# Shares of layer-2 tiles per chunk, and which tiles of the last stretch are split, in a two-layer graph kernel

## The chip, the cores and the metric

The kernel runs on one core of one Trainium2 chip. The metric is the device time of one execution in microseconds (us); the median of three runs is given. Changes of about 0.2% of it (some 3.7 us) can be told from none.

## What is computed

`x` is 8192 x 128, `adj` 8192 x 8192, all f32. The reference, cut to what matters:

```
h = relu(layernorm(x))
h1 = h @ W + B
mask = (adj < 0.5) & ~eye
S = where(mask, exp(-(1/adj - 1/mu)**2 / (2*sigma**2)), 0)
x = x + S @ h1                                   # layer 1
h2 = relu(layernorm(x)) @ W1.T
x = x + (adj*adj + eye) @ h2                     # layer 2
```

## The kernel before

**Tiles.** The 8192 rows are 16 chunks of 512. `adj` is read as 16 x 16 tiles (row chunk, source chunk), each 128 partitions x 2048 f32, 1 MB. A tile is used in layer 1 and in layer 2. Layer 2 of a tile (row, source) needs `h2` of its source chunk, and that is known only when layer 1 of that chunk is done, so most tiles are loaded twice. A tile is four steps of 128 rows on TensorE (PE); a plain f32 matmul stands in the trace as two records, so a plain tile is eight.

**Steps and chunks.** Step s = 16 c + i is the i-th layer-1 tile of chunk c; there are 256 such steps (LAST = 240 is the first of the last chunk), and then 34 more with layer-2 tiles alone. The 256 layer-2 tiles ("items", numbered m = 0 to 255 in the order in which every engine does them) are put beside the steps. `QUOTA[c]` (L31) says how many items go beside chunk c; the last chunk takes what is left. `make_plan` (L86) spreads them over the 16 steps of the chunk and collects them in chains: tiles of one row that add up in one PSUM bank, which VectorE (DVE) then copies out (`add_chain`, L722) and GpSimd (POOL) adds to the output by DMA. In the last chunk three items stand beside most steps, in some steps two.

**A layer-1 tile.** DVE masks it (`premask`, L607, the instruction at L619), ScalarE (ACT) takes log (L801) and reciprocal (L806), DVE squares (L626), ACT takes the exponential (L811), and PE multiplies three steps later (`l1`, L440, L449). In the last chunk `premask(t)` waits until PE has done `l1(t-3)`, because the ring of results has three places there.

**A layer-2 tile.** Its entries are squared in place, by DVE (L637) or ACT (L819; in the last chunk always ACT), and PE multiplies by `h2` (L483). A diagonal tile also gets the unit matrix added by DVE (L604).

**Split tiles.** In the last stretch some items are split by DVE into a high part (L658) and a low part (L660, both in `halves`, L648); PE then does three fast matmuls for each step of 128 rows (L461 to L463, twelve records for a tile) in place of the plain ones. `SPLITS` (L172) chooses them by a rule of the index:

```
SPLITS = [it for it in ITEMS if it.step >= LAST + SPLIT_STEP.get(it.source, STEPS) and it.row != it.source
          and it.m % 7 not in (1, 4)]
```

DVE splits item m when it comes to item m+1. So the last item of a step is split in the next step, behind that step's `premask`:

```
for it in AT_STEP[s]:
    if dense and it is AT_STEP[s][0]:
        premask(s)
    ...
    if it.m and ITEMS[it.m - 1].split is not None:
        halves(ITEMS[it.m - 1])
```

PE goes through step s as `l1(s-3)`, then the items of step s-1. At the start of a chunk `centre_row(c-1)` (L518) stands behind the chunk's first `l1`; it waits for `add_x1(c-1)` on DVE (L696), which is queued behind a square and a `premask` of that step.

**Loads.** SP loads tiles in the order of use into a ring of eight places; a place is free when PE is done with the item that was in it.

Of the kernel before, what the change touches and what calls it, by code (L numbers as in the profile page):

```python
# [27 lines left out]

QUOTA = [0, 11, 13] + [12] * 3 + [13] * 9  # L31
S_STEPS = NC * NC
H2_STEP = 6

# [3 lines left out]
LAST = S_STEPS - NC  # L38
# [6 lines left out]
SPLIT_STEP = {10: 3, 11: 3, 13: 5, 12: 7, 14: 12, 15: 16}  # L45
# [22 lines left out]
def slots_of(c):  # L68

    if c == 1:  # L70
        n = QUOTA[1]
        first = H2_STEP - 1
        return [first + k * (NC - first) // n for k in range(n)]
    if c < NC - 1:
        n = QUOTA[c]
        return [(2 * k + 1) * NC // (2 * n) for k in range(n)]
    n = NC * NC - 2 * NC + 1 - sum(QUOTA) - len(KEPT)
    return [(2 * k + 1) * NC // (2 * n) for k in range(n)]
# [70 lines left out]
CHAINS, ITEMS, ORDER = make_plan()  # L149
STEPS = ITEMS[-1].step + 1  # L150
# [8 lines left out]
for s in range(STEPS):  # L159
# [3 lines left out]
    for it in AT_STEP[s]:  # L163
# [3 lines left out]
        else:  # L167
# [1 line left out]
            LOADS.append((None, it))  # L169


SPLITS = [it for it in ITEMS if it.step >= LAST + SPLIT_STEP.get(it.source, STEPS) and it.row != it.source  # L172
          and it.m % 7 not in (1, 4)]
for it in ITEMS:
    it.split = None
for r, it in enumerate(SPLITS):
    it.split = r
# [62 lines left out]
def gnn_program(nc, xT, adjT, W0, B0, mu, sigma, W1T, outT):  # L240
    with ExitStack() as ctx:
# [332 lines left out]
        def _(dve):  # L574
# [74 lines left out]
            def halves(it):  # L649
# [6 lines left out]
                else:  # L656
                    dve.wait_ge(q_used, SPLITS[it.split - 3].m + 1)
                dve.tensor_copy(high[:, :], squares).then_inc(high_ready, 1)  # L658
# [295 lines left out]
```

## Time and profile before

| | us |
| --- | --- |
| median of 3 runs (1869.32 to 1871.13) | 1870.15 |
| the profiled execution | 1871.51 |
| its span, first to last instruction | 1869.6 |
| PE busy | 1835.1 (98%) |
| DVE busy | 1743.2 (93%) |
| ACT busy | 1731.2 (93%) |
| DMA, mean over the span | 271 GB/s |

All times of the rows below are from the start of the span. "Busy" of PE is taken with matmuls that overlap and with modelled ends; the distance from start to start of two records is the surer measure of what one costs.

### The profile page before, as it was taken

Reading aid. Unit: us, or ns where it says so; the run is one execution under the profiler, and the core shown is the slowest. Engines: PE = TensorE matmul, PEld = TensorE weight load, DVE = VectorE, ACT = ScalarE, POOL = GpSimd, SP = SyncE. Lnnn points to the kernel's source line nnn. Section 1 sums busy time; section 2 is a strip of 40 time slices with the busy share of each in tenths; the row PEclk is TensorE's granted clock in tenths of the full one; section 3 lists DMA queues with packets and bytes.
Section 4 is the critical chain, followed back from the end, with each engine's and each line's share of the span. In section 5 each row is a group of like instructions: output and inputs, shape, how many; then the busy total and the mean of one; then the engine's idle time right before and its main releaser. Section 6 shows DMA issues by size and latency. Waiting matters only on the chain.

```text
span 1869.6 us, 13360 instructions
## 1 busy us (share of the span) xinstructions
PE 1835.1 (98%) x4836; PEld 884.6 (47%) x4836; DVE 1743.2 (93%) x1029; ACT 1731.2 (93%) x985; POOL 96.1 (5%) x118
## 2 busy tenths in 40 slices
PE   7989999999999999999999999999999999999998
PEld 4544444444444444444444444444444444555665
DVE  7999999999999999999999998999999994778796
ACT  8999899999999999999999999999999998888664
POOL 0000000000000000000000000000000000000111
PEclk9999999999999999999999999999999999999999
DMA  8476889897978787777878776676756678866998
GB/s 315 162 288 257 319 305 308 288 324 246 330 267 316 261 298 278 276 279 275 284 263 304 237 247 241 249 255 228 255 200 232 232 265 297 291 253 229 311 339 250
DMA packets 85297, 507.29 MB, mean 271 GB/s; under 512 B 9840, under 2 KB 10480, under 8 KB 28144
## 3 DMA queue, kind: packets, MB, share of 16 engines
q1 hardware_dynamic: 69840, 476.68, 67.0%
q0 software_dynamic: 15248, 29.63, 9.2%
q8 instruction: 39, 0.64, 0.1%
q14 instruction: 26, 0.21, 0.0%
q10 hardware_dynamic: 144, 0.13, 0.0%
HBM read 476.51 MB, written 29.88 MB: 271 GB/s over the span
## 4 chain that ended last, share of the span: by engine, by line
PE 76%; DVE 11%; ACT 8%; issue 3%; DMA 1%; SPq 0%; DVEq 0%
PE p_x L483 21%; PE p_l1b L449 20%; PE p_l1a L449 15%; PE p_own L483 11%; DVE rings L626 4%; DVE rings L619 3%; ACT rings L801 3%; DVE rings L637 2%; ACT rings L811 2%; ACT rings L806 2%; PE p_l1a L483 1%; PE p_x L461 1%; PE p_x L462 1%; PE p_x L463 1%; PE p_own L461 1%
## 5 line engine op out<-in xcount | busy, mean ns | idle before, releaser
L619 DVE SCALAR_TENSOR_TENSOR rings<-rings 128x2048 f32<-128x2048 f32 x256 | 584.6, 2284 | 35.9 <-PE p_l1b L449 31.0
L626 DVE SCALAR_TENSOR_TENSOR rings<-rings,small 128x2048 f32<-128x2048 f32 x256 | 599.9, 2344 | 14.4 <-ACT rings L806 14.2
L811 ACT ACTIVATE rings<-rings,small 128x2048 f32<-128x2048 f32 x256 | 533.1, 2082 | 47.0 <-DVE rings L626 46.5
L801 ACT ACTIVATE rings<-rings,small 128x2048 f32<-128x2048 f32 x256 | 509.6, 1991 | 15.3 <-DVE rings L619 11.6
L483 PE MATMUL p_x<-rings,h 128*128 128x512 f32 x1144 | 513.3, 592 | 0.0
L806 ACT ACTIVATE rings<-rings 128x2048 f32<-128x2048 f32 x256 | 488.0, 1906 | 5.6
L449 PE MATMUL p_l1b<-rings,h 128*128 128x512 f32 x1024 | 461.2, 596 | 0.0
L449 PE MATMUL p_l1a<-rings,h 128*128 128x512 f32 x1024 | 458.4, 593 | 0.7 <-DVE h L687 0.7
L483 PEld LDWEIGHTS p_x<-rings,h 128*128 128x128 f32 x1144 | 216.8, 190 | 266.3 <-issue 264.8
L637 DVE TENSOR_TENSOR rings<-rings 128x2048 f32<-128x2048 f32 x136 | 310.4, 2282 | 1.6
L449 PEld LDWEIGHTS p_l1b<-rings,h 128*128 128x128 f32 x1024 | 195.2, 191 | 240.7 <-issue 237.6
L449 PEld LDWEIGHTS p_l1a<-rings,h 128*128 128x128 f32 x1024 | 193.1, 190 | 235.7 <-issue 233.4
L819 ACT ACTIVATE rings<-rings 128x2048 f32<-128x2048 f32 x120 | 224.8, 1900 | 38.3 <-DMA rings<-adjT 28.1
L483 PE MATMUL p_own<-rings,h 128*128 128x512 f32 x520 | 233.6, 592 | 0.0
L920 POOL DMA_DIRECT2D outT<-xa_buf x97 | 82.5, 853 | 1422.0 <-DVE xa_buf L737 1409.4
L483 PEld LDWEIGHTS p_own<-rings,h 128*128 128x128 f32 x520 | 98.6, 190 | 120.0 <-issue 119.5
L660 DVE TENSOR_TENSOR low<-rings,high 128x2048 fp32r<-128x2048 f32 x41 | 94.0, 2292 | 1.4
L737 DVE COPY xa_buf<-p_x 128x512 f32<-128x512 f32 x86 | 58.6, 682 | 17.2 <-PE p_x L483 17.2
L658 DVE CAST high<-rings 128x2048 fp32r<-128x2048 f32 x41 | 50.0, 1221 | 12.4 <-ACT rings L819 12.4
L461 PE MATMUL p_x<-high,h_high 128*128 128x512 f32 x92 | 41.4, 450 | 0.5 <-DVE low L660 0.5
L463 PE MATMUL p_x<-high,h_low 128*128 128x512 f32 x92 | 35.9, 390 | 0.0
L462 PE MATMUL p_x<-low,h_high 128*128 128x512 f32 x92 | 35.9, 390 | 0.0
(92 smaller groups left out, 571.0 us busy)
## 6 DMA issues: line engine op xcount, KB each, us to landing
rings<-adjT SPq DMA_DIRECT2D x446, 1024.0 KB, 6.9
outT<-xa_buf POOLq DMA_DIRECT2D x97, 256.0 KB, 7.3
x_buf<-xT SPq DMA_DIRECT2D x24, 256.0 KB, 6.4
outT<-y_buf POOLq DMA_DIRECT2D x15, 256.0 KB, 7.5
xa_buf<-xT SPq DMA_DIRECT2D x8, 256.0 KB, 5.6
outT<-x_buf POOLq DMA_DIRECT2D x1, 256.0 KB, 5.0
y_buf<-outT SPq DMA_DIRECT2D x1, 256.0 KB, 12.6
outT<-y_buf SPq DMA_DIRECT2D x1, 128.0 KB, 1.8
```

The source lines that it names most:

```text
L449: last = pe.matmul(p_l1[c % 2][:, :], h1[:, J * G + g, :], block_of(s_ring, slot_of(t), g), start=(i == 0 and g == 0), stop=(i == NC - 1 a ...
L461: pe.matmul(out[:, :], h_high, high, start=(it.first and g == 0), stop=False)
L483: last = pe.matmul(out[:, :], h2[:, it.source * G + g, :], block_of(a_ring, it.load % A_RING, g), start=(it.first and g == 0), stop=(it.la ...
L619: dve.scalar_tensor_tensor(out=tile(s_ring, slot_of(t)), in0=tile(a_ring, slot), scalar=CUTOFF, in1=tile(a_ring, slot), op0=ALU.is_lt, op1 ...
L626: dve.scalar_tensor_tensor(out=v, in0=v, scalar=neg_2c, in1=v, op0=ALU.add, op1=ALU.mult).then_inc(squared, 1)
L637: squares = dve.tensor_tensor(a, a, a, ALU.mult)
L660: dve.tensor_tensor(low_ring[it.load % A_RING][:, :], squares, high[:, :].bitcast(F32), ALU.subtract).then_inc(low_ready, 1)
L801: act.activation(v, v, ACT.Ln, bias=tiny_c).then_inc(ln_done, 1)
L806: act.activation(v, v, ACT.Exp, scale=-1.0).then_inc(recip_done, 1)
L811: act.activation(v, v, ACT.Exp, bias=exp_bias, scale=neg_k).then_inc(sens_done, 1)
L819: squares = act.activation(a, a, ACT.Square)
L920: pool.dma_start(columns(outT, ch.row), xa_buf[ch.index % XA_RING][:, :], accum_op=how).then_inc(xa_stored[ch.index % XA_RING], 16)
```

## The change

```
-QUOTA = [0, 11, 13] + [12] * 3 + [13] * 9
+QUOTA = [0, 11, 13, 11, 14, 12, 14, 12, 13, 13, 12, 14, 12, 12, 12]
...
-SPLITS = [it for it in ITEMS if it.step >= LAST + SPLIT_STEP.get(it.source, STEPS) and it.row != it.source
-          and it.m % 7 not in (1, 4)]
+MAY_SPLIT = [it for it in ITEMS if it.step >= LAST + SPLIT_STEP.get(it.source, STEPS) and it.row != it.source]
+WHICH = "SSSSSSSSSSS.SSS..SSSS.SS.S.SSSSSS.S.SS.S.SS.SSSS.SS.SSSSSS"
+SPLITS = [it for it, w in zip(MAY_SPLIT, WHICH) if w != "."]
```

Chunk 3 gets 11 items for 12, chunk 4 14 for 12, chunk 6 14 for 13, chunk 7 12 for 13, chunk 10 12 for 13, chunk 11 14 for 13, chunks 12, 13 and 14 each 12 for 13, and the last chunk 47 for 45. 45 tiles are split in place of 41: 22 for 18 beside the last chunk's steps (seven for four in steps 243 to 247, fifteen for fourteen in steps 248 to 255), and 23 in both kernels in the 34 steps behind it, at other places. There are 97 chains for 98. Lines behind L172 stand one further down.

The first place is DVE in steps 253 and 254. L619 (now L620) is `premask`, L626 (L627) the square of a layer-1 tile, L658 and L660 (L659, L661) the high and the low part of a split tile, L604 (L605) a unit matrix, L737 (L738) a copy of a chain. Before, from the `premask` of step 253:

```order
L619 SCALAR_TENSOR_TENSOR rings<-rings 128x2048
L658 CAST high_57<-rings 128x2048
L660 TENSOR_TENSOR low_51<-rings,high_57 128x2048
L626 SCALAR_TENSOR_TENSOR rings<-rings,small 128x2048
L619 SCALAR_TENSOR_TENSOR rings<-rings 128x2048
L658 CAST high_58<-rings 128x2048
L660 TENSOR_TENSOR low_52<-rings,high_58 128x2048
L658 CAST high_59<-rings 128x2048
L660 TENSOR_TENSOR low_55<-rings,high_59 128x2048
L737 COPY xa_buf<-p_l1a 128x512
L658 CAST high_57<-rings 128x2048
L660 TENSOR_TENSOR low_54<-rings,high_57 128x2048
```

The changed kernel, from the `premask` of step 253:

```order
L620 SCALAR_TENSOR_TENSOR rings<-rings 128x2048
L605 TENSOR_TENSOR rings<-rings,eye 128x4x128
L659 CAST high_58<-rings 128x2048
L661 TENSOR_TENSOR low_52<-rings,high_58 128x2048
L659 CAST high_59<-rings 128x2048
L661 TENSOR_TENSOR low_51<-rings,high_59 128x2048
L627 SCALAR_TENSOR_TENSOR rings<-rings,small 128x2048
L620 SCALAR_TENSOR_TENSOR rings<-rings 128x2048
L738 COPY xa_buf<-p_l1a 128x512
L659 CAST high_57<-rings 128x2048
L661 TENSOR_TENSOR low_55<-rings,high_57 128x2048
L659 CAST high_58<-rings 128x2048
```

Before, step 253 has two items, the last of them split: its parts are the first pair behind the `premask` of step 254, followed by the pairs of that step's own two split items. Now step 253 has three items, the last of them plain, and behind the `premask` of step 254 come a copy and the pairs of that step's own items.

The second place is DVE at steps 262 to 266, in the part without layer 1. L703 (L704), L710 (L711), L668 and L670 (L669, L671) belong to the layer norm and `h2` of the last chunk. Before, from that layer norm's first row:

```order
L703 TENSOR_SCALAR normed_buf<-p_stat 128x512
L658 CAST high_57<-rings 128x2048
L660 TENSOR_TENSOR low_50<-rings,high_57 128x2048
L710 TENSOR_TENSOR h<-p_proj,rstd_columns 128x512
L668 CAST h_high_70<-h 128x512
L670 TENSOR_TENSOR h_low_71<-h,h_high_70 128x512
L658 CAST high_58<-rings 128x2048
L660 TENSOR_TENSOR low_52<-rings,high_58 128x2048
L658 CAST high_59<-rings 128x2048
L660 TENSOR_TENSOR low_53<-rings,high_59 128x2048
L737 COPY xa_buf<-p_x 128x512
L658 CAST high_57<-rings 128x2048
```

The changed kernel, from the same row:

```order
L704 TENSOR_SCALAR normed_buf<-p_stat 128x512
L659 CAST high_58<-rings 128x2048
L661 TENSOR_TENSOR low_50<-rings,high_58 128x2048
L659 CAST high_59<-rings 128x2048
L661 TENSOR_TENSOR low_51<-rings,high_59 128x2048
L711 TENSOR_TENSOR h<-p_proj,rstd_columns 128x512
L669 CAST h_high_70<-h 128x512
L671 TENSOR_TENSOR h_low_71<-h,h_high_70 128x512
L659 CAST high_57<-rings 128x2048
L661 TENSOR_TENSOR low_53<-rings,high_57 128x2048
L738 COPY xa_buf<-p_x 128x512
L659 CAST high_58<-rings 128x2048
```

Before, the pairs behind the layer norm are those of items 227, 229, 230 and 231 (steps 261, 263, 264, 265). Now they are those of items 227, 228, 230 and 232 (steps 261, 262, 264, 266): two pairs stand ahead of `h2` for one, and items 229 and 231 are plain.

## Rows read from the trace of the kernel before

**Rows 1.** Page: busy time and share of the span; granted PE clock, tenths, 40 slices.

```profile
PE 1835.1 (98%) x4836; PEld 884.6 (47%) x4836; DVE 1743.2 (93%) x1029; ACT 1731.2 (93%) x985; POOL 96.1 (5%) x118
...
PEclk9999999999999999999999999999999999999999
```

**Rows 2.** Windows (length, busy by engine, clock, DMA share, GB/s): chunk 3, last chunk, rest.

```profile
334.60:434.80 100.20, 99.14 (x243) 44.60 (x242) 99.56 (x54) 97.67 (x54) 6.56 (x8) 1.00 0.84 293
...
1573.70:1760.90 187.20, 184.62 (x540) 101.50 (x539) 144.14 (x90) 153.91 (x85) 9.26 (x11) 0.99 0.77 275
1760.90:1862.90 102.00, 100.44 (x375) 68.60 (x373) 87.56 (x67) 55.67 (x32) 17.92 (x18) 1.00 0.95 308
```

**Rows 3.** Timeline of PE (start, us, line, [idle before]) at the starts of chunks 4, 5.

```profile
440.69 1.13 PE L518 MATMUL p_stat<-x_buf,centre_w 128*128 128x512 f32 x2 [2.27 <-DVE x_buf L696]
...
449.28 1.16 PE L533 MATMUL p_proj<-w,normed_buf 128*128 128x128 f32 x8 [0.59 <-DVE normed_buf L703]
...
541.22 1.13 PE L518 MATMUL p_stat<-x_buf,centre_w 128*128 128x512 f32 x2 [0.61 <-DVE x_buf L696]
```

**Rows 4.** Groups of chunk 3 (334.6 to 434.8): ACT's exponential, busy, mean ns, idle before.

```profile
L811 ACT ACTIVATE rings<-rings,small 128x2048 f32<-128x2048 f32 x16 | 33.3, 2082 | 1.8 <-DVE rings L626 1.7
```

**Rows 5.** Timeline of DVE at the start of chunk 4.

```profile
435.49 2.35 DVE L626 SCALAR_TENSOR_TENSOR rings<-rings,small 128x2048 f32<-128x2048 f32 x1
437.76 2.28 DVE L619 SCALAR_TENSOR_TENSOR rings<-rings 128x2048 f32<-128x2048 f32 x1
439.96 0.68 DVE L696 TENSOR_TENSOR x_buf<-p_l1b,x_buf 128x512 f32<-128x512 f32 x1
```

**Rows 6.** Timeline of PE, items of steps 252 and 253.

```profile
1702.77 3.60 PE L483 MATMUL p_l1a<-rings,h 128*128 128x512 f32 x8
...
1708.95 0.47 PE L461 MATMUL p_x<-high,h_high 128*128 128x512 f32 x1
...
1711.80 3.59 PE L449 MATMUL p_l1b<-rings,h 128*128 128x512 f32 x8
1715.23 3.60 PE L483 MATMUL p_x<-rings,h 128*128 128x512 f32 x8
1721.40 0.47 PE L461 MATMUL p_own<-high,h_high 128*128 128x512 f32 x1 [2.58 <-DVE low L660]
...
1725.73 1.53 PE L449 MATMUL p_l1b<-rings,h 128*128 128x512 f32 x3
```

**Rows 7.** Timeline of DVE: premask of step 254 and item 215's low part.

```profile
1715.51 2.29 DVE L619 SCALAR_TENSOR_TENSOR rings<-rings 128x2048 f32<-128x2048 f32 x1 [4.43 <-PE p_l1b L449]
...
1718.97 2.29 DVE L660 TENSOR_TENSOR low<-rings,high 128x2048 fp32r<-128x2048 f32 x1
```

**Rows 8.** Windows, columns as in 2: granted clock behind the idle of 1721.40.

```profile
1723.00:1725.00 2.00, 2.00 (x6) 1.52 (x6) 2.00 (x2) 1.97 (x2) 0.00 (x0) 0.50 0.00 0
```

**Rows 9.** Timeline of PE: the longest idle behind the start.

```profile
138.84 1.87 PE L524 MATMUL p_stat<-mean_of,square_buf 128*128 128x1 f32 x8 [3.60 <-ACT square_buf L843]
```

**Rows 10.** Timeline of PE, items 228, 230, 231 and within split items 233 and 234.

```profile
1777.83 3.59 PE L483 MATMUL p_l1a<-rings,h 128*128 128x512 f32 x8
...
1784.77 0.47 PE L461 MATMUL p_x<-high,h_high 128*128 128x512 f32 x1 [0.50 <-DVE low L660]
...
1788.83 0.47 PE L461 MATMUL p_own<-high,h_high 128*128 128x512 f32 x1 [1.06 <-DVE low L660]
...
1795.33 0.40 PE L462 MATMUL p_x<-low,h_high 128*128 128x512 f32 x1
...
1798.06 0.39 PE L462 MATMUL p_x<-low,h_high 128*128 128x512 f32 x1
```

**Rows 11.** Timeline of ACT, squares of items 250 and 255 (each starts as its load lands).

```profile
1836.30 1.92 ACT L819 ACTIVATE rings<-rings 128x2048 f32<-128x2048 f32 x1 [1.74 <-DMA rings<-adjT]
...
1851.42 1.92 ACT L819 ACTIVATE rings<-rings 128x2048 f32<-128x2048 f32 x1 [1.53 <-DMA rings<-adjT]
```

**Rows 12.** Windows, columns as in 2: the DMA late in the tail.

```profile
1820.00:1840.00 20.00, 20.00 (x76) 13.89 (x75) 17.30 (x13) 12.10 (x7) 3.10 (x3) 1.00 1.04 377
```

## The prediction

> **What bounds the kernel now.** I read the page first. PE is busy in 98% of the span, DVE and ACT in 93%, and the granted clock is 9 tenths or more in all 40 slices [rows 1]. That looks like a kernel in which PE sets the time and nothing else can help. But "busy" joins matmuls whose ends are modelled, so I went to windows by chunk, and then to the starts of PE's records. In the last chunk PE is short of its window by 2.6 us (187.20 against 184.62), and in the rest by 1.6 us [rows 2]. Chunk 3 is different: DVE is busy for 99.56 of 100.20 us, more than PE [rows 2]. So there are two kinds of place: long ones in which PE works without a break, where only less PE work counts, and a few in which PE waits for DVE, where the order on DVE counts.
>
> The prices, from start to start. A plain tile is 3.43 us (1711.80 to 1715.23) [rows 6]. A split tile is 2.73 us (the same record of twelve, 1795.33 to 1798.06) [rows 10]. On DVE a square of layer 1 is 2.27 us and a premask 2.20 us [rows 5]. A pair of split parts runs from the premask's end (1715.51 + 2.20 = 1717.71) to the low part's (1718.97 + 2.29 = 1721.26), 3.5 us, all of it on DVE [rows 7].
>
> **The change part by part.** Sums are made on the profiled execution, 1871.51 us, with a span of 1869.6. The median of the runs, 1870.15, is 1.36 below it; I move it by the same sum.
>
> *Four more split tiles.* Their number is 45 for 41, the other tiles are the same in all, and PE does them all. PE saves 4 x (3.43 - 2.73) = 2.8 us. DVE gives 4 x 3.5 = 14 us for it. Three of the four lie in steps 243 to 247. DVE waits for PE there often: the last chunk holds 43 us in which DVE is not busy [rows 2], and that is the cover. Without it they would cost 3.5 us each. Two more tiles stand beside the last chunk and two fewer ahead of it; where PE works without a break, moving one costs nothing: 3.43 us less there, 3.43 us more here.
>
> *The wait at item 215.* PE's longest wait in the last chunk is at 1721.40, idle 2.58 by the row, and 2.74 from starts (1715.23 + 3.43 = 1718.66) [rows 6]. Its cause is the order. Step 253 has two items and the second is split. DVE may split it only behind the premask of step 254, and that waits until PE has ended the layer-1 tile of 1711.80, and starts at 1715.51; premask and pair end at 1721.26 [rows 7]. Meanwhile PE has one plain tile to do, 3.43 us, for a path of about 5.9. A step of three items whose last is split shows no wait: from 1702.77 to 1708.95 PE does one plain and one split tile, 6.18 us, where 3.43 + 2.73 = 6.16 [rows 6]. In the new order every step of the last chunk with two items ends in a plain one, and steps 244, 248, 249, 250 and 255, which end in a split one, have three. The wait goes: -2.7. Late next is nothing near: the pairs of step 254's own items stand one place earlier than before.
>
> *The half clock behind it.* From 1721.40 to 1725.73 that split tile takes 4.33 us in place of 2.73 [rows 6], and the granted clock is 0.50 of full speed, the lower level, 1.2 GHz, at 1723 to 1725 [rows 8]. What PE did before it fell was to stand idle for 2.7 us. With the idle gone I take this off as well: -1.7 (1.6 in this tile, 0.1 in the next).
>
> *A small new wait in step 244.* It now ends in two split items, and step 245 has a layer norm, a sum and a split of `h2` ahead of its premask. By my sum of the queue DVE ends the last pair 0.3 us after PE could use it: +0.3, between 0 and 3.5 (a whole pair late).
>
> *Items 229 to 231.* Before, three split tiles stand in a row behind the late `h2` of the last chunk, and PE waits twice, 0.50 and 1.06 by the rows [rows 10], 0.66 and 1.22 from starts. Now 228 is split and 229 and 231 are plain. From 1777.83 [rows 10] PE needs 2.73 for 228 and 3.43 for 229 and comes to 230 at 1783.99; before, its pair was ready at 1784.6, just ahead of the 1784.77; one pair less (3.5) stands ahead of it, and of the new pair of 228 about 1.6 lies outside the time in which DVE waited for the layer norm, so it is ready at 1782.7. Then PE comes to 232 at 1783.99 + 2.73 + 3.43 = 1790.1, and DVE, behind the copy of a chain that PE ends at 1784.0, has it ready at 1784.7 + 3.5 = 1788.2. Both waits go: -1.9.
>
> *Items 248 to 252.* Five split tiles in a row are new. I carry the same clock on. From 230 to 250 there are 15 split and 6 plain tiles: 41.0 + 20.6 = 61.5 us, so PE comes to item 251 at 1845.5. DVE can begin on 250 when ACT has squared it, 1836.30 + 1.92 = 1838.2 [rows 11], ends at 1841.9, copies a chain (0.6), and ends 251 at 1845.9 and 252 at 1849.3. PE waits 0.4 and then 0.7: +1.1.
>
> *Chunks 3 to 5.* PE waits 2.27 and 0.59 us at the start of chunk 4 and 0.61 at that of chunk 5 (2.43, 0.76 and 0.78 from starts), each time for DVE [rows 3]: the sum of chunk 3 is queued behind a square and a premask, and nothing between them is idle [rows 5]. One tile less in chunk 3 takes 3.4 us from PE, but only 2.2 (a square) and 0.6 (a copy) from DVE, 2.8 in all. ACT keeps all its work, and was idle for only 1.8 us before its exponentials there [rows 4]. So the wait at 440.69 grows, by 0.6 if DVE sets the chunk and by 2.0 if ACT does. I take 1.3, between them, as the two are chained tile by tile. Chunk 4 then has 14 tiles, 6.9 us more for PE and 2.2 more for DVE: DVE gets 4 us ahead, and the wait at 541.22 goes (-0.8). Together +0.5. In chunks 6 to 14 PE does not wait before and has at most 3.5 us less to do in one chunk; the lead of DVE, up to 8 us, covers that.
>
> *A half clock at chunk 4.* The trace has idles of 3.60 [rows 9] and 2.58 that were followed by the lower clock, and 2.27 that was not. The grown wait is 3.6. By these rows I expect a fall there, at the price of the short one: +1.7, between 0 and 3.4 (two such stretches).
>
> Sum: -2.8 - 2.7 - 1.7 + 0.3 - 1.9 + 1.1 + 0.5 + 1.7 = -5.5. The profiled execution would take 1866.0, the median **1864.7 us**.
>
> **The rivals.**
>
> *The clock does not fall at chunk 4.* Only one row speaks for a fall at such a length, and the 2.27 us idle shows that there is a lower end. All else as above: 1870.15 - 7.2 = 1863.0. The Trainium skill (TensorE: Matmul & The Clock Gate, "What's actually happening") says that the monitor of PE's activity runs free and doesn't start with the kernel. By it the same idle may or may not be followed by a fall; the trace has one execution and can't show it.
>
> *The wait at 215 comes back elsewhere.* Five steps end in a split tile with no more than 0.2 us of room. If one of them gets a wait of the old size with its half clock, 4.4 us come back: 1869.1, no change. For it speaks step 244; against it, that steps of the same make show none.
>
> *DVE becomes the bound beside the last chunk (slower).* Each step with two split tiles gives DVE 2.2 + 2 x 3.5 + 2.3 + a copy = 12.0 us and PE 2 x 3.43 + 2 x 2.73 = 12.3. If DVE comes late to the premasks by more than 0.2 us, all five steps that end in a split tile wait for what is over. It turns the sum to slower by 0.2% at (5.5 + 3.7)/5 + 0.2 = 2.0 us late; at 2.5 late it costs 5 x 2.3 = 11.5: 1876.2. Against it speaks DVE's idle time in that chunk.
>
> *The loads set the tail.* The last loads land 3.0 us apart (1836.30 to 1851.42 for five) [rows 11], a tile takes PE 2.73 or 3.43, and the DMA moves 377 GB/s with all its engines busy [rows 12]. If the loads come no earlier and PE catches up with them, what the tail gains (0.8) is lost and about 1 more: 1866.5. Item 255 is 1851.42 + 1.92 ready but for a unit matrix, some 4 us ahead of PE, which speaks against it. The Trainium skill (DMA: Bandwidth & Descriptors, "Where 436 GB/s comes from") puts the limit of one core's HBM at about 358 GB/s. By that rule these windows could not be reached, and the loads would set the tail already before; the trace, with 377, doesn't agree, and PE has no idle in that window.
>
> That the change doesn't do what it says is ruled out: the order shows 45 tiles split and 97 chains.
>
> **How the numbers follow.** The forecast, 1864.7, has 0.38; no fall of the clock, 1863.0, 0.28; the wait elsewhere, 1869.1, 0.21; DVE as the bound, 1876.2, 0.06; the loads, 1866.5, 0.07. A measurement can tell about 0.2%, 3.7 us, from no change, so faster is below 1866.4. The first two give 0.66, and I add half of the loads' and of the third case's near side: 0.74. Same is 0.20, slower 0.06. The range is 1860.8 to 1868.8: below 1863.0 by the 2.2 that chunk 3 and the two small waits may spare, above the forecast by 4.1, for a pair late in step 244 or most of a wait like that at 215.
>
> **What the profile would show.** Right: no idle of PE above 1 us behind the start of the last chunk, none before items 230 and 231, short ones before 251 and 252, and PE busy some 3 us less. At chunk 4 an idle of 3 to 4 us before L519 with a lower clock behind it, and none at chunk 5. Wrong: idle of PE for L661 in steps 244 to 250, a DVE that is never idle beside the last chunk, or an idle at chunk 4 of 5 us and more, since then ACT or DVE would hold the early chunks and the quotas would cost what the last chunk saves.

## The result, and the profile after

| | before | after |
| --- | --- | --- |
| median, us (six runs each) | 1871.25 (1869.32 to 1872.51) | 1859.49 (1858.25 to 1860.58) |
| the profiled execution | 1871.51 | 1858.25 |
| its span | 1869.6 | 1856.5 |
| start of chunk 3 | 334.6 | 333.6 |
| start of chunk 6 | 640.1 | 640.1 |
| start of the last chunk | 1573.7 | 1563.4 |
| end of PE | 1862.9 | 1850.1 |

The changed kernel takes 0.9938 of the time before (95%: 0.9926 to 0.9951), 11.8 us less. The forecast was 5.5 less, and its range ended at 1860.8. The direction held, the size did not.

The page of the changed kernel, the lines of [rows 1]:

```profile
PE 1829.9 (99%) x4852; PEld 887.5 (48%) x4852; DVE 1752.3 (94%) x1034; ACT 1733.4 (93%) x987; POOL 95.4 (5%) x117
...
PEclk8999999999999999999999999999999999999999
```

PE's busy time falls by 5.2 us (1835.1 to 1829.9), yet the span falls by 13.1. So more than half of the gain is time in which PE was idle, and the page cannot say where. It needs the windows. Those of the changed kernel, with the columns of [rows 2]: chunk 3, chunk 4, the last chunk, and the rest up to the end of PE:

```profile
333.60:435.20 101.60, 99.49 (x244) 44.46 (x243) 100.14 (x54) 99.69 (x55) 5.71 (x7) 1.00 0.82 294
435.20:537.90 102.70, 102.48 (x252) 46.33 (x251) 102.53 (x57) 100.84 (x56) 7.76 (x9) 1.00 0.84 288
...
1563.40:1750.40 187.00, 187.00 (x572) 106.27 (x571) 159.70 (x103) 158.90 (x87) 9.69 (x11) 1.00 0.80 287
1750.40:1850.10 99.70, 99.70 (x374) 68.75 (x372) 87.67 (x67) 55.44 (x32) 17.64 (x17) 1.00 0.95 314
```

From the start of the last chunk on, PE is busy for 286.7 of 286.7 us, where before it lacked 4.1 in those two windows [rows 2]. DVE is busy for 159.70 us beside the last chunk, 15.6 more than the 144.14 before, and still has 27 us over. Chunk 3 got a tile less and lasts longer, 101.60 us for 100.20. Its ACT is busy for 99.69 us, 2.0 more than before.

The timeline of PE in the changed kernel: five places in chunks 3 to 5, the last item of step 253 with the layer-1 tile behind it, and three tiles from the part behind layer 1:

```profile
338.30 1.13 PE L519 MATMUL p_stat<-x_buf,centre_w 128*128 128x512 f32 x2 [1.07 <-DVE x_buf L697]
...
414.48 3.70 PE L450 MATMUL p_l1b<-rings,h 128*128 128x512 f32 x8 [1.03 <-ACT rings L812]
...
438.62 1.02 PE L519 MATMUL p_stat<-x_buf,centre_w 128*128 128x512 f32 x2
...
447.62 1.05 PE L525 MATMUL p_stat<-mean_of,square_buf 128*128 128x1 f32 x8 [0.22 <-ACT square_buf L844]
...
541.32 1.02 PE L519 MATMUL p_stat<-x_buf,centre_w 128*128 128x512 f32 x2
...
1711.82 3.59 PE L484 MATMUL p_x<-rings,h 128*128 128x512 f32 x8
1715.25 3.60 PE L450 MATMUL p_l1b<-rings,h 128*128 128x512 f32 x8
...
1770.01 3.60 PE L484 MATMUL p_x<-rings,h 128*128 128x512 f32 x8
...
1776.17 3.59 PE L484 MATMUL p_own<-rings,h 128*128 128x512 f32 x8
1779.20 0.79 PE L462 MATMUL p_l1a<-high,h_high 128*128 128x512 f32 x1
```

The wait of 2.27 at the start of chunk 4 is gone, with both waits of 0.6 that followed it. In their place PE waits 1.03 for ACT (1.20 from starts) at 414.48 and 0.22 (0.38) at 447.62. The end of step 253 goes from a plain tile straight into the next `l1` (1711.82 and 1715.25, 3.43 apart), where item 215 had waited 2.6 [rows 6]. Items 229 and 231 (1770.01, 1776.17) are plain, and the split tiles 230 (between them) and 232 (at 1779.20) start without an idle, where [rows 10] had 0.50 and 1.06. The wait at the start of chunk 3 (1.07) is none of the change: the kernel before has one of 1.06 there.

**The account of the profiled executions**, from the starts in the table and the waits:

| stretch | PE work | waits and half clock | sum |
| --- | --- | --- | --- |
| up to chunk 3 | 0 | | -1.0 |
| chunks 3 to 5 (37 tiles for 36) | +3.4 | 3.97 to 1.58: -2.4 | +1.0 |
| chunks 6 to 14 (114 tiles for 117) | -10.3 | 0 | -10.3 |
| from the last chunk on (two tiles more, four more split) | +6.9 - 2.8 | -2.7 - 1.7 - 1.9 | -2.5 measured (-2.2 by the sum) |
| behind PE's last matmul (8.6 to 8.1 of the profiled execution) | | | -0.5 |

The moved tiles cancel (3.4 - 10.3 + 6.9). What is left is -2.8 for split tiles, -2.4 in chunks 3 to 5, -4.4 at item 215, -1.9 at items 230 and 231, -1.0 before chunk 3, -0.5 at the end and 0.3 that the terms leave open. The -1.0 is chance: in ten profiles of kernels that are alike up to there, chunk 3 starts between 332.7 and 334.8. Most of it goes with an idle of PE in chunk 1 [rows 9], which is 3.6 us in some of these profiles and 3.1 in others, of kernels with the old quotas and with the new: where it is 3.6, chunks 1 and 2 take 208.2 to 208.4 us, and where it is 3.1, 206.1 to 207.4. The profiled run also was the lowest of its six, 1.2 below their median, so the -13.3 of the two profiled runs and the -11.8 of the medians tell the same.

### The profile page after: what moved, and what is told of

The parts are those of the page before. It is cut to its first block, busy times and chain, and to the rows that moved or that the text cites. A ratio compares the mean times of both kernels' runs of the same rounds, so it can differ in the third digit from the quotient of the medians.

```text
span 1856.5 us, 13400 instructions
## 1 busy us (share of the span) xinstructions
PE 1829.9 (99%) x4852; PEld 887.5 (48%) x4852; DVE 1752.3 (94%) x1034; ACT 1733.4 (93%) x987; POOL 95.4 (5%) x117
## 4 chain that ended last, share of the span: by engine, by line
PE 82%; ACT 11%; DVE 5%; issue 2%; DMA 0%; DVEq 0%; ACTq 0%
PE p_x L484 22%; PE p_l1b L450 21%; PE p_l1a L450 18%; PE p_own L484 11%; ACT rings L802 4%; ACT rings L812 3%; ACT rings L807 3%; DVE rings L620 2%; DVE rings L627 2%; PE p_x L462 1%; PE p_x L464 1%; PE p_x L463 1%; DVE rings L638 1%; PE p_l1a L484 1%; PE p_stat L525 1%
## 5 line engine op out<-in xcount | busy, mean ns | idle before, releaser
L627 DVE SCALAR_TENSOR_TENSOR rings<-rings,small 128x2048 f32<-128x2048 f32 x256 | 600.0, 2344 | 17.3 <-ACT rings L807 17.1
L620 DVE SCALAR_TENSOR_TENSOR rings<-rings 128x2048 f32<-128x2048 f32 x256 | 584.5, 2283 | 18.0 <-PE p_l1b L450 14.9
L484 PE MATMUL p_x<-rings,h 128*128 128x512 f32 x1128 | 506.1, 592 | 0.0
L638 DVE TENSOR_TENSOR rings<-rings 128x2048 f32<-128x2048 f32 x134 | 305.9, 2283 | 2.8
L661 DVE TENSOR_TENSOR low<-rings,high 128x2048 fp32r<-128x2048 f32 x45 | 103.1, 2292 | 1.5
L738 DVE COPY xa_buf<-p_x 128x512 f32<-128x512 f32 x85 | 57.9, 682 | 16.1 <-PE p_x L484 16.1
L659 DVE CAST high<-rings 128x2048 fp32r<-128x2048 f32 x45 | 55.0, 1221 | 12.8 <-ACT rings L820 11.9
```

The lines of the kernel that those rows point to most:

```text
L484: last = pe.matmul(out[:, :], h2[:, it.source * G + g, :], block_of(a_ring, it.load % A_RING, g), start=(it.first and g == 0), stop=(it.la ...
L620: dve.scalar_tensor_tensor(out=tile(s_ring, slot_of(t)), in0=tile(a_ring, slot), scalar=CUTOFF, in1=tile(a_ring, slot), op0=ALU.is_lt, op1 ...
L627: dve.scalar_tensor_tensor(out=v, in0=v, scalar=neg_2c, in1=v, op0=ALU.add, op1=ALU.mult).then_inc(squared, 1)
L638: squares = dve.tensor_tensor(a, a, a, ALU.mult)
L661: dve.tensor_tensor(low_ring[it.load % A_RING][:, :], squares, high[:, :].bitcast(F32), ALU.subtract).then_inc(low_ready, 1)
```

## The experiments

Three kernels take the change apart, two more look at chunks 3 and 4 alone, three at the marks alone, and three follow a wait that both kernels have. Ratios are to the kernel before, on the same chip. "Against after" is the difference of medians to 1859.49. That compares runs made at different times, most of them on different chips, and each ratio has an interval of 1.7 to 2.4 us to either side, so that a difference of 3 us against after is not shown by the medians alone; where it is read below, the stretches of the traces carry it. The stretch "last chunk to end" is from its first matmul to PE's end: 289.2 us before, 286.7 after.

**The new quotas alone, with the old rule of the index** (which then splits 43 tiles):

```
-QUOTA = [0, 11, 13] + [12] * 3 + [13] * 9
+QUOTA = [0, 11, 13, 11, 14, 12, 14, 12, 13, 13, 12, 14, 12, 12, 12]
```

> The kernel before with the new QUOTA and its old rule m % 7; the rule now hits 43 tiles, and step 253 has three items, two of them plain or ahead of the split last one. Theory A (the quotas do two things: they take PE's waits at the starts of chunks 4 and 5, and by giving step 253 a third item they end the wait at item 215 with its half clock; the marks only add the rest): faster than before by 2.4 + 4.4 + 2 x 0.7 = 8.2 us, PE idle at the start of chunk 4 under 0.5 us, none at item 215, the two idles before items 230 and 231 (0.5 and 1.1) still there. Theory B (the marks do the most): faster by at most 3 us.

Measured: 1864.02 us (1863.28 to 1864.73), ratio 0.9968 (0.9955 to 0.998), 6.7 less than before. Step 253 has three items in this plan, and there is no wait at its end. The waits of chunks 3 and 4 are those of after (1.23, 1.2, 0.38). The tail keeps its two waits (0.66 at 1777.45 and 1.22 at 1781.51, from starts), and there are new ones. Timeline of PE:

```profile
1689.71 0.47 PE L461 MATMUL p_l1a<-high,h_high 128*128 128x512 f32 x1 [0.49 <-DVE low L660]
...
1781.51 0.47 PE L461 MATMUL p_own<-high,h_high 128*128 128x512 f32 x1 [1.06 <-DVE low L660]
```

So the quotas alone bring over half of the change: the wait at 215 (4.4), chunks 3 to 5 (2.4) and two split tiles (1.4), less 1.0 for new waits at 1689.71 (0.65 from starts) and 1773.99 (0.39); 7.2 by this sum. The marks bring the other 4.5: two split tiles (1.4) and the four waits (0.65 + 0.39 + 0.66 + 1.22 = 2.9), 4.3 by the sum. The forecast of this run, 8.2, had none of the new waits and counted each of the parts as here.

**In the kernel before, item 214 split in place of 215** (41 as before):

```
-          and it.m % 7 not in (1, 4)]
+          and (it.m % 7 not in (1, 4) or it.m == 214) and it.m != 215]
```

> The kernel before, with item 214 split in place of 215: the same 41 split tiles, and step 253 (two items) ends in a plain one. Theory A (the wait comes from the order on DVE, premask of step 254 ahead of the pair of 215, and the half clock follows the idle): faster by 2.7 + 1.7 = 4.4 us, no PE idle in the last chunk above 0.3 us and no stretch of 0.50 clock there. Theory B (DVE is short of time there, and the wait only moves to another tile of steps 253 to 255): 0 to 1 us, and a new PE idle of 2 us or more behind DVE's low part. Theory C (the clock falls for another reason): 2.7 us, and the 0.50 stretch stays.

Measured: 1866.71 us (1865.39 to 1867.72), ratio 0.9979 (0.997 to 0.9988), 4.1 less; last chunk to end 285.2 us, 3.9 less. Timeline of PE:

```profile
439.73 1.13 PE L518 MATMUL p_stat<-x_buf,centre_w 128*128 128x512 f32 x2 [2.26 <-DVE x_buf L696]
440.69 5.29 PE L483 MATMUL p_x<-rings,h 128*128 128x512 f32 x8
...
540.31 1.08 PE L518 MATMUL p_stat<-x_buf,centre_w 128*128 128x512 f32 x2
...
1717.01 3.60 PE L483 MATMUL p_own<-rings,h 128*128 128x512 f32 x8
1720.44 1.02 PE L449 MATMUL p_l1b<-rings,h 128*128 128x512 f32 x2
```

At 1717.01 a plain tile of 3.43 us ends the step, with no wait and no half clock. One mark is worth 4.1 us, more than all four added split tiles: the wait was set by the order on DVE, as the prediction had it. The start of chunk 4 shows something new: the same idle as before, 2.26, is followed by a tile of 5.29 us here. The window behind it:

```profile
442.00:444.00 2.00, 2.00 (x4) 0.97 (x3) 1.97 (x3) 1.05 (x1) 0.00 (x0) 0.50 0.99 125
```

The clock has fallen to 0.50, 1.2 GHz, for 3.4 us. Yet the two later waits (0.59 and 0.61 in [rows 3]) are gone, and chunk 3 to chunk 6 take 305.5 us, to a tenth what they take before. DVE sets the time there, and a slow PE only uses up what it would have waited. The profile of the next run shows the same a second time: idle 2.26 at 438.98, the clock at 0.50 behind it, no later wait, and 305.5 us.

**In the kernel before, the new marks from item 222 on alone** (23 split tiles there in both):

```
-          and it.m % 7 not in (1, 4)]
+          and (it.m in {223, 224, 226, 227, 228, 230, 232, 233, 235, 237, 238, 240, 241, 242, 243, 245,
+              246, 248, 249, 250, 251, 252, 254} if it.m >= 222 else it.m % 7 not in (1, 4))]
```

> The kernel before, with the new marks for the items from 222 on (23 split tiles in both). Theory A (the loads come earlier when PE frees their places earlier, so five split tiles in a row find their data in time): both idles before items 230 and 231 go and none comes, 1.9 us faster. Theory B, the one of my forecast (loads land when they landed before): a new wait of 0.4 and 0.7 before items 251 and 252, 0.8 us faster.

Measured: 1869.46 us (1867.48 to 1871.36), ratio 0.9994 (0.9985 to 1.0003). By the medians that is 1.3 less and not told from nothing. The trace tells more: last chunk to end takes 287.0 us, 2.1 less, and the four tiles behind `h2` follow each other without an idle. Timeline of PE, items 229 and 230 (the start of a split tile that PE takes without a wait is drawn 0.4 ahead of the end of the plain one):

```profile
1778.81 3.59 PE L483 MATMUL p_x<-rings,h 128*128 128x512 f32 x8
1781.84 0.79 PE L461 MATMUL p_x<-high,h_high 128*128 128x512 f32 x1
```

No wait stands before items 251 and 252 either, where the prediction had 1.1 us.

**In the changed kernel, 12 and 13 tiles beside chunks 3 and 4** (for 11 and 14; 98 chains):

```
-QUOTA = [0, 11, 13, 11, 14, 12, 14, 12, 13, 13, 12, 14, 12, 12, 12]
+QUOTA = [0, 11, 13, 12, 13, 12, 14, 12, 13, 13, 12, 14, 12, 12, 12]
```

> The changed kernel with QUOTA 12 and 13 for chunks 3 and 4 in place of 11 and 14; their sum and all from chunk 5 on keep their numbers of tiles. Theory A (11 and 14 take PE's waits, since chunk 4 puts a tile at its step 1, ahead of the wait at its start, while DVE has a square and a copy less before it): PE idle of 2 to 3 us again at the start of chunk 4, 2 to 2.5 us slower than the changed kernel. Theory B (the profile's difference there is chance, or the gain comes from the later quotas): the same as the changed kernel within 0.7 us, and PE idle at chunk 4 below 1 us.

Measured: 1862.16 us (1861.52 to 1864.17), ratio 0.9958 (0.9946 to 0.9971), 2.7 against after. Chunk 3 to chunk 6 take 310.2 us for the same 37 tiles, 3.7 more than after. The granted clock is 0.50 from 447.8 on for 3.4 us. Timeline of PE:

```profile
447.98 2.08 PE L534 MATMUL p_proj<-w,normed_buf 128*128 128x128 f32 x8 [3.12 <-DVE normed_buf L704]
```

The wait is one step later and larger, and the half clock follows it. The order shows why it is there: in this plan the third step of chunk 4 (step 66) has no item, so PE has nothing to do between the two matmuls of the row of chunk 3 (L519 and L534) but one layer-1 tile; the changed kernel has item 37 there. Not all of the 3.7 is the edit's: 0.6 is a longer wait at the start of chunk 3 (1.67 for 1.07), behind chunks 1 and 2 that passed 1.3 us quicker in this profile. From chunk 1 to chunk 6 it takes 2.5 us more than after, near the 2.7 of the medians. So 11 and 14 in place of 12 and 13 are a part of the gain, where the prediction had booked a loss.

**In the kernel before, 11 and 13 tiles beside chunks 3 and 4:**

```
-QUOTA = [0, 11, 13] + [12] * 3 + [13] * 9
+QUOTA = [0, 11, 13, 11, 13, 12, 13, 13, 13, 13, 13, 13, 13, 13, 13]
```

> The kernel before with QUOTA 11 and 13 for chunks 3 and 4 in place of 12 and 12; their sum, all later chunks and all 41 split tiles stay. Theory A (a tile that moves from chunk 3 to an early step of chunk 4 leaves PE's work before the wait at chunk 4 as it was and takes work from DVE): the waits at the starts of chunks 4 and 5, 4.0 us with what follows them, shrink to some 1.6, 2.4 us faster, no half clock there. Theory B, my forecast's (PE gets to the wait 3.4 us earlier and DVE only 2.8): the wait grows to 3.6 us and a half clock follows; same or slower by up to 2 us.

Measured: 1871.35 us (1870.15 to 1873.46), ratio 1.0002 (0.9993 to 1.0011): nothing in all. Chunk 3 to chunk 6 do take 1.1 us less (304.4), with waits of 1.20 at 415.54 and 1.70 at 445.72 for the 3.97 of before. Theory A had 2.4: the wait at the row sum goes as it said, but with 13 tiles beside chunk 4 step 66 has no item, and PE waits 1.70 behind it where the changed kernel waits 0.38. And the items are numbered through, and the rule of the index then splits all three of step 251. Timeline of PE:

```profile
1696.71 0.47 PE L461 MATMUL p_l1a<-high,h_high 128*128 128x512 f32 x1 [1.75 <-DVE low L660]
```

The new wait at 1696.71 (1.9 from starts) and one of 0.6 at 1851.88 take the gain back. This run says little on the quotas by its total. It shows why the marks are written one by one: with a rule of the index, a move in chunk 3 changes the order in the last one.

**In the changed kernel, the old marks from item 222 on:**

```
+OLD = {223, 224, 226, 227, 229, 230, 231, 233, 234, 236, 237, 238, 240, 241, 243, 244, 245, 247, 248,
+       250, 251, 252, 254}
-SPLITS = [it for it, w in zip(MAY_SPLIT, WHICH) if w != "."]
+SPLITS = [it for it, w in zip(MAY_SPLIT, WHICH) if (it.m in OLD if it.m >= 222 else w != ".")]
```

> The changed kernel with the old marks for the items from 222 on. Theory A: the waits before items 230 and 231 come back, 0.7 and 1.2 us, 1.9 slower than the changed kernel. Theory B (loads that land at fixed times): 0.8 us slower.

Measured: 1862.17 us (1859.73 to 1862.31), ratio 0.995 (0.9937 to 0.9962), 2.7 against after; last chunk to end 289.3 us, 2.6 more. Timeline of PE:

```profile
1774.67 0.47 PE L463 MATMUL p_x<-high,h_high 128*128 128x512 f32 x1 [0.47 <-DVE low L662]
...
1778.72 0.47 PE L463 MATMUL p_own<-high,h_high 128*128 128x512 f32 x1 [1.06 <-DVE low L662]
```

The two waits of [rows 10] are back, 0.63 and 1.22 from starts, and 0.33 at 1840.64. They are 2.2 of the 2.6; the rest is in gaps too short to name.

**In the changed kernel, four tiles less split** (185, 189, 193 and 196, of steps 243 to 247; 41 in all):

```
-SPLITS = [it for it, w in zip(MAY_SPLIT, WHICH) if w != "."]
+SPLITS = [it for it, w in zip(MAY_SPLIT, WHICH) if w != "." and it.m not in (185, 189, 193, 196)]
```

> The changed kernel with items 185, 189, 193 and 196 plain: 41 split tiles, the number of before. Theory A (PE sets the time and DVE has room): 4 x 0.70 = 2.8 us slower than the changed kernel, DVE 14 us less busy and its idle up by that. Theory B (the four are not on the path): no difference.

Measured: 1862.52 us (1862.36 to 1863.72), ratio 0.9956 (0.9943 to 0.9968), 3.0 against after; last chunk to end 289.5 us, 2.8 more. Window of the last chunk:

```profile
1564.70:1754.00 189.30, 189.30 (x556) 103.34 (x554) 146.21 (x95) 158.92 (x87) 9.66 (x11) 1.00 0.79 283
```

The 2.8 us of the prediction are met. DVE has 13.5 us less to do (146.21 for 159.70; forecast 14), and PE is without a break in both. The four pairs lie in time that DVE had free.

**In the changed kernel, four tiles more split** (204, 209, 215 and 218; 49 in all):

```
-SPLITS = [it for it, w in zip(MAY_SPLIT, WHICH) if w != "."]
+SPLITS = [it for it, w in zip(MAY_SPLIT, WHICH) if w != "." or it.m in (204, 209, 215, 218)]
```

> The changed kernel with items 204, 209, 215 and 218 split as well, 49 in all: steps 250, 253 and 254 have three split tiles in a row, 15.5 us of DVE work each against 11.6 us of PE work. Theory A (DVE has about 0.3 us of room in each step with two, none for a third): PE saves 4 x 0.7 = 2.8 but waits 0.5 us or more for the last tile of steps 250, 253 and 254 and more in the steps behind them, where premask comes late; in sum 3 to 8 us slower than the changed kernel, and the waits stand before split tiles. Theory B (DVE has the idle time to take them): 2.8 us faster.

Measured: 1872.39 us (1869.85 to 1875.05), ratio 1.0009 (1.0 to 1.0018), 12.9 against after. Timeline of PE, and windows of the last chunk and behind two of its waits:

```profile
1677.79 0.76 PE L462 MATMUL p_own<-high,h_high 128*128 128x512 f32 x1 [2.96 <-DVE low L661]
...
1720.49 0.47 PE L462 MATMUL p_x<-high,h_high 128*128 128x512 f32 x1 [3.55 <-DVE low L661]
...
1736.66 0.77 PE L462 MATMUL p_x<-high,h_high 128*128 128x512 f32 x1 [4.29 <-DVE low L661]
```

```profile
1564.10:1753.00 188.90, 177.39 (x556) 105.93 (x555) 166.02 (x107) 154.27 (x85) 8.93 (x10) 0.97 0.76 268
1678.00:1680.00 2.00, 2.00 (x5) 1.57 (x6) 1.97 (x3) 2.00 (x2) 0.97 (x1) 0.50 1.00 422
1721.00:1723.00 2.00, 2.00 (x10) 1.62 (x9) 1.97 (x2) 2.00 (x2) 0.96 (x1) 1.00 1.03 434
```

Waits for `low` come to 12.8 us (3.13, 3.71, 4.45, 0.90, 0.62 from starts), a wait for a unit matrix to 0.86, and the half clock behind two of them to 4.5: 18.2 in all, less 2.8 for the four tiles is 15.4, against 15.8 seen in last chunk to end. DVE is busy for 166 of 189 us and has 23 over. It does not become the bound by the sum of its work; it comes late at three places in the order. The loss was forecast at 3 to 8, and was larger, for the waits came at up to 4.5 us each. The profiled execution, 1875.05, is the slowest of eleven (1869.85 to 1875.05), so the typical loss is nearer the 12.9 of the medians. The changed kernel stands close to such a place: four more tiles of the kind that saved 2.8 cost 12.9.

**A wait that both kernels have.** In chunk 1 PE stands idle for ACT's squares of a layer norm for 3.60 us [rows 9], and works at the lower clock behind it. Of the changed kernel, the timeline and a window:

```profile
138.14 1.87 PE L525 MATMUL p_stat<-mean_of,square_buf 128*128 128x1 f32 x8 [3.08 <-ACT square_buf L844]
139.87 9.31 PE L450 MATMUL p_l1b<-rings,h 128*128 128x512 f32 x16
```

```profile
141.00:143.00 2.00, 2.00 (x4) 0.88 (x3) 2.00 (x2) 2.00 (x2) 0.00 (x0) 0.50 0.75 315
```

Two edits to the changed kernel, each alone and then both. The first gives ACT the squares of items 6 and 21 (from DVE):

```
-        it.by = "act" if it.m % (5 if it.step < 4 * NC else 4) == 3 and it.row != it.source else "dve"
+        it.by = "act" if (it.m % (5 if it.step < 4 * NC else 4) == 3 or it.m in (6, 21)) and it.row != it.source else "dve"
```

> The changed kernel with items 6 and 21 (chunks 1 and 2) squared by ACT in place of DVE. Theory A (up to the start of chunk 4 DVE sets the time, and PE's waits there only show it): DVE has 4.4 us less to do before the wait at the start of chunk 3, ACT 3.6 more of which it idles 4.5 now; the wait of 1.2 us there goes, and the 1.2 us for ACT in chunk 3 stays or grows to 2.4: 0.5 to 2 us faster than the changed kernel. Theory B (DVE is not on the path there): no difference.

The second puts the row of variances one step later in chunk 1:

```
-                if i == 4 and c < NC - 1 or i == 6 and c == NC - 1:
+                if i == (5 if c == 1 else 4) and c < NC - 1 or i == 6 and c == NC - 1:
```

> The changed kernel with PE's variance matmuls of the first row (L525) one step later, behind the next layer-1 tile. Now PE stands idle 3.1 us before them and then runs 6.8 us at half clock, 6.5 us in all. Theory A (DVE sets the time until chunk 4): the idle and the half clock go or shrink, and PE waits as much longer at the starts of chunks 2 to 4: no difference within 1 us. Theory B (PE sets the time there too): 4 to 6 us faster.

> Both edits in the changed kernel. Theory A: with DVE relieved of 4.4 us, the part of PE's early loss that DVE hid begins to count; 2 to 4 us faster than the changed kernel. Theory B (ACT is at its limit as well): as act_early.

| us | median | ratio (95%) | chunk 1 to 3 | chunk 3 to 6 |
| --- | --- | --- | --- | --- |
| after | 1859.49 | 0.9938 (0.9926 to 0.9951) | 207.3 | 306.5 |
| squares to ACT | 1858.21 | 0.9927 (0.9914 to 0.9941) | 208.4 | 304.7 |
| variances later | 1858.55 | 0.9936 (0.9923 to 0.9948) | 206.6 | 307.2 |
| both | 1854.95 | 0.9914 (0.99 to 0.9927) | 205.0 | 304.7 |

With the first edit alone the wait at the start of chunk 3 goes, and chunk 3 to 6 take 1.8 us less. Chunk 1 to 3 take 1.1 more, but this profile has the 3.6 us idle in chunk 1, and 208.4 is what the others with it take. The median is 1.3 below after, inside the 0.5 to 2 of theory A and not told from nothing.

The second edit does what it says. Timeline of PE:

```profile
139.53 0.95 PE L525 MATMUL p_stat<-mean_of,square_buf 128*128 128x1 f32 x8
...
337.85 1.12 PE L519 MATMUL p_stat<-x_buf,centre_w 128*128 128x512 f32 x2 [1.76 <-DVE x_buf L697]
```

The idle of 3.1 before L525 is gone, and with it the half clock, which had taken some 3.4 us of PE (6.8 us at the lower clock). And nothing is gained: chunk 1 to 6 take 513.8 us as in after. PE waits at 337.85 for 1.76 where after has 1.07, and for ACT in between. With both edits PE and DVE are relieved together, and 4.2 us go from that stretch (509.7). PE no longer waits at the start of chunk 3. Window with both:

```profile
126.70:435.00 308.30, 304.47 (x744) 137.23 (x743) 304.75 (x171) 301.48 (x165) 20.91 (x30) 1.00 0.83 296
```

PE, DVE and ACT are each busy for over 301 of the 308.3 us. By the medians the version with both edits is 4.5 us faster than the changed kernel. But the two were measured at different times, and their intervals overlap (0.99 to 0.9927 and 0.9926 to 0.9951); the two profiled executions are 2.5 us apart, since the 4.2 us won up to chunk 6 are partly lost at the start and the end. So the gain over after is likely rather than shown, and the 4.2 us of that stretch speak for it.

## Why the prediction was right in direction and wrong in size

The gap is 7.8 us on the profiled executions (-5.5 forecast, -13.3 measured). Chunks 3 to 5 make 4.6 of it, waits that did not come 1.4, chance before chunk 3 1.0, the end behind PE 0.5, and 0.3 is left open. The end behind PE is chance too (8.1 to 8.7 us in the same ten profiles); the two make up the 1.5 by which the profiled executions are further apart than the medians.

**"Chunks 3 to 5" and "a half clock at chunk 4": the step that failed.** The text was: "One tile less in chunk 3 takes 3.4 us from PE, but only 2.2 (a square) and 0.6 (a copy) from DVE". It was booked at +0.5 and +1.7; measured is -2.4. The shares are counted by chunk, but the wait is not at a chunk's end. It is in the order a few items behind the first tile of chunk 4, and with 14 tiles in that chunk its second step has an item that it had not with 12. So one item less in chunk 3 is made up by one more ahead of the wait. Groups of the kernel before from 339 to 439, about from the row sum of chunk 2 to that of chunk 3, PE's and DVE's:

```profile
L449 PE MATMUL p_l1b<-rings,h 128*128 128x512 f32 x120 | 53.5, 593 | 0.0
L483 PE MATMUL p_x<-rings,h 128*128 128x512 f32 x80 | 36.0, 592 | 0.0
L483 PE MATMUL p_own<-rings,h 128*128 128x512 f32 x16 | 7.2, 592 | 0.0
...
L637 DVE TENSOR_TENSOR rings<-rings 128x2048 f32<-128x2048 f32 x10 | 22.8, 2282 | 0.0
L737 DVE COPY xa_buf<-p_x 128x512 f32<-128x512 f32 x7 | 4.8, 680 | 0.0
```

The same groups of the changed kernel:

```profile
L450 PE MATMUL p_l1b<-rings,h 128*128 128x512 f32 x120 | 53.6, 594 | 1.0 <-ACT rings L812 1.0
L484 PE MATMUL p_x<-rings,h 128*128 128x512 f32 x80 | 36.0, 592 | 0.0
L484 PE MATMUL p_own<-rings,h 128*128 128x512 f32 x16 | 7.2, 592 | 0.0
...
L638 DVE TENSOR_TENSOR rings<-rings 128x2048 f32<-128x2048 f32 x9 | 20.5, 2283 | 0.2
L738 DVE COPY xa_buf<-p_x 128x512 f32<-128x512 f32 x6 | 4.1, 680 | 0.0
```

PE has the same work, 96 records of layer 2, which are twelve tiles in both. DVE has one square and one copy less: item 35, the last beside chunk 3 before, is now the first beside chunk 4, where the kernel gives ACT every fourth square in place of every fifth, and a chain less ends ahead of the sum. So DVE, which is what PE waited for, has 2.8 us less to do. It waits for ACT 0.6 us longer, and its sum of chunk 3 starts 99.7 us behind that of chunk 2 (337.56 to 437.29), where it was 101.5 (338.51 to 439.96): 1.7 earlier. No run gives only the square of item 35 back to DVE, so what it is worth by itself (2.2 of the 2.8, by its price) is worked out and not tested. Timeline of DVE in the changed kernel:

```profile
437.29 0.69 DVE L697 TENSOR_TENSOR x_buf<-p_l1b,x_buf 128x512 f32<-128x512 f32 x1
```

The sum is done at 437.98, ahead of PE's 438.62. Before, it started at 439.96 [rows 5]. The price stands on ACT, which the prediction named as the other end. Timeline of ACT, the exponential for the 14th layer-1 tile of chunk 3 before, then that of the changed kernel with ACT's next square:

```profile
413.95 2.08 ACT L811 ACTIVATE rings<-rings,small 128x2048 f32<-128x2048 f32 x1
```

```profile
412.35 2.08 ACT L812 ACTIVATE rings<-rings,small 128x2048 f32<-128x2048 f32 x1
...
422.05 1.89 ACT L820 ACTIVATE rings<-rings 128x2048 f32<-128x2048 f32 x1
```

Counted from the chunk's first tile, it ended at 81.5 us and now ends at 80.8. PE did that layer-1 tile at 83.1 before (417.66), and with a tile less ahead of it could do it at 79.7. It waits 1.2 us for ACT, at 414.48. Here the tile less in chunk 3 does what the prediction had said; the square that ACT has more comes later (422.05) and is not what PE waits for. That wait brings PE to L519 1.2 us later and DVE's sum comes 1.7 earlier, more than the 2.43 of before. The waits of 0.76 and 0.78 behind it go as well, for one of 0.38, which with the 2.43 gone and the 1.20 come makes the -2.4.

With no idle before L519 there is nothing for a half clock to follow. The +1.7 was also booked without asking whether PE sets the time there: in the two profiles in which the clock fell at this wait with the old shares (the swapped mark and the new tail marks), chunks 3 to 5 take the same 305.5 us, because two later waits go. With 12 and 13 tiles there is no later wait that could go, and the fall does count: of the 3.7 us more, 0.6 is the wait at chunk 3 and 1.7 the longer waits (3.29 for 1.58, from starts), which leaves 1.4 for it. The two runs on the shares of chunks 3 and 4 alone bear out that this stretch hangs on them, by +3.7 (0.6 of it another wait) and -1.1. Both ends that the prediction gave the grown wait (+0.6 and +2.0) were losses, though no reason excluded a gain, and so the range ended too early.

**Four more split tiles, -2.8: right.** The run with four tiles less split gave 2.8 in the trace and 3.0 by the medians, under the cover that was named.

**The wait at item 215 and the half clock behind it, -4.4: right.** The run that swapped one mark gave -3.9 in the trace and -4.1 by the medians.

**A small new wait in step 244, +0.3: none came.** DVE ends the low part of the step's last item just ahead of PE. Timeline of the changed kernel, DVE and then PE:

```profile
1597.54 2.29 DVE L661 TENSOR_TENSOR low<-rings,high 128x2048 fp32r<-128x2048 f32 x1
```

```profile
1599.98 0.47 PE L462 MATMUL p_x<-high,h_high 128*128 128x512 f32 x1
```

The pair ends at 1599.83 and PE takes it at 1599.98: 0.15 us of room where the sum had 0.3 too late. That is within what such a sum can tell.

**Items 229 to 231, -1.9: right, by its steps.** The pairs end 0.1 us from where they were carried to: that of 230 at 1772.3, which is 1782.8 in the frame of before (item 228 starts at 1767.29 for 1777.83), for 1782.7; that of 232 at 1777.8, or 1788.3, for 1788.2. The two runs with one set of tail marks each gave -2.1 and +2.6.

**Items 248 to 252, +1.1: wrong.** PE comes to item 251 as forecast (1834.93, or 1845.5 in the frame of before), but its pair is ready 1.4 us earlier than carried. The error is the load: the sum let ACT square item 250 at 1836.30 as before. Timeline of ACT in the changed kernel:

```profile
1822.60 1.92 ACT L820 ACTIVATE rings<-rings 128x2048 f32<-128x2048 f32 x1 [0.55 <-DMA rings<-adjT]
```

Item 250 is squared at 1822.60, 1833.2 in the frame of before, 3.1 earlier; the pair gains only 1.4 of it, as DVE is then still at the pair of item 249. A load starts when PE is done with the item that was in its place. With the waits before 230 and 231 gone, PE frees the places earlier, and the loads move up with PE. Other runs bear it out: counted from PE's last matmuls for the variances, item 250 is squared 62.2 us on before, and 62.5 and 63.4 with the old tail marks in the two runs with the new quotas, but 59.0 in the changed kernel and with the new tail marks alone. A landing time of the old run is no fixed date.

**The rivals.** "The clock does not fall at chunk 4" came true, but for another reason than chance: there was no idle. "The wait comes back elsewhere" and "DVE becomes the bound" did not happen in the change; the latter is what the run with 49 split tiles shows, at the predicted kind of place and above the predicted price. "The loads set the tail" has nothing for it: the window behind layer 1 has no idle of PE at 314 GB/s.

## What to carry to other kernels

When work is moved between stages, count what stands ahead of the actual wait in each engine's order, on the engine that waits and on the one that is waited for, and don't go by the stage's totals: here a tile "less" left PE's work ahead of the wait as it was and took 2.8 us from DVE's. On a nearly full engine one item at the wrong place in a neighbour's order (4.1 us for the mark of item 215, 12.9 for four marks too many) is worth more than four items made cheaper (2.8). And where two engines alternate as the bound, as in chunk 1, relieving one of them may show little or nothing until the other is relieved too (0 for PE alone, at most 1.8 us for DVE alone, 4.2 for both).

## What the runs showed of the hardware

The lower clock does not follow from the length of the last idle alone. The idle at the start of chunk 4, 2.27 us before and 2.26 with the swapped mark, had no fall behind it in the one profile and 3.4 us at 0.50 in the other, in code that is the same up to there; with the new tail marks it had the fall again. The idle of 2.58 at item 215 was followed by the fall in all three profiles that have it. In the run with 49 split tiles idles of 2.96 and 4.29 us were followed by the lower clock, and one of 3.55 between them was not. The Trainium skill (TensorE: Matmul & The Clock Gate, "What's actually happening") says that the monitor of PE's activity runs free. By that rule the same idle may or may not be followed by a fall, and these profiles agree.

A half clock is not a loss where another engine sets the time: at chunk 4, with the old shares, it cost nothing in 305.5 us, and in chunk 1 its removal, alone, gained nothing. Where PE had no slack, behind item 215, it cost 1.7.
